# The rank features of a shared pass computed by quarters of its tokens, in the bank of the odd group's sums

## Chip, cores and metric

The kernel runs on one core of one Trainium2 chip. The metric is the device time of one execution in microseconds (us); lower is better.

## What is computed

The input is read as 2048 rows of 512. Each row is normalised, goes through an attention against a context, is added back and normalised again. A mixture of experts follows: each of the 2048 rows (tokens) goes to two of eight experts, and a shared expert sees all of them. Every expert, the shared one too, has a second, narrow branch of rank 32. For the shared one:

```python
sh = gelu(xt @ sw1 + sb1) @ sw2 + sb2      # 512 -> 2048 -> 512
sh = sh + gelu(xt @ swd) @ swu             # 512 -> 32 -> 512
out = out + 0.2 * sh
```

The change touches `gelu(xt @ swd)`, the rank features of the shared expert.

## The kernel before

**Staging.** Tokens are handled in 16 groups of 128. The first part of the kernel, up to about 640 us, runs attention and the shared expert together; the second part runs the eight experts. The shared expert works in 9 passes over tokens: pass 0 has group 0, passes 1 to 7 have groups 2p-1 and 2p (256 tokens), pass 8 has group 15. Between two passes lies a window of two groups' attention.

**Order.** Each of the five engines has its own program, and all walk the same list of units that `work_order()` writes out by hand. What an engine doesn't take part in it skips; what it does take part in it runs strictly in list order, waiting on semaphores. A pass p puts these units in the list, with pieces of attention between them: `rank` (the rank features), 16 times `up` (a block of 128 hidden features), and later `down` (hidden features times second weights). Just behind the second `up` the list has the last `values` unit of the odd group 2p+1 (L1776) and then its `ones` unit (L1785).

**Sums of the softmax.** For groups in `SUMMED` (2 and 4 to 15) VectorE adds up the exponentials in float32 (L1399, `late_stage`, 128x1024, in pairs of heads), and `ones` multiplies the total by a block of ones on TensorE. It waits for the last of those additions (`s_sum`). The result of an odd group goes to PSUM bank 3, that of an even group to bank 5. `den` reads it (L1411).

**A value in two parts.** Products run in bf16 with each float32 operand split into a high and a low part: three products for one. The rank weights are `wdh` and `wdl`. Before, each was stored three times side by side (96 columns, `WIDE`), so that one matmul gave three copies of the features on partitions 0 to 95 (L1822, 12 matmuls of 256 columns in a pass). ScalarE took the Gelu of all three copies at once (L1184), VectorE made the high part of all with one cast (L1487), and the low part of the middle copy with one subtraction (L1489). The tile `low` then holds high, low, high for `down` (L1849).

**The experts' way.** The rank features of the eight experts are already computed by quarters of the slots: 48 matmuls of 32 weight columns by 160 slots, each quarter on 32 partitions of its own (L1908), four Gelus (L1234), two casts and a subtraction (L1492, L1493, L1495).

**Banks.** `rank`, `up`, `down` and even `turn` units took PSUM banks 6 and 7 in turns (the function `shared_bank` waits for the reader of the unit that had the bank before). In the last `up` units of pass 7 and in pass 8 the ring is 6, 7, 0, 1. So before, the second `up` of a pass had the bank of `rank` and waited for its Gelu (`s_rgelu`).

Of the kernel before, what the change touches and what calls it, by code (L numbers as in the profile page):

```python
# [9 lines left out]
F32 = mybir.dt.float32  # L10
# [512 lines left out]
def build(nc, x, ctx_in, itok, gate_w, w1, b1, w2, b2, wd, wu, sw1, sb1, sw2, sb2, swd, swu, out):  # L523
    stack = ExitStack()
    with stack:
# [18 lines left out]
        wdf = sb("wdf", [P, KB, RANK], F32)  # L544
        wdh, wdl = sb("wdh", [P, KB, WIDE], BF16), sb("wdl", [P, KB, WIDE], BF16)
        wuf_turned, wus = sb("wuf_turned", [P, D], F32), sb("wus", [P, D], BF16)
# [6 lines left out]
        low = [sb(f"low{i}", [P, SLOTS], BF16) for i in range(2)]  # L553
        lowf = sb("lowf", [WIDE, SLOTS], F32)
        yout = [sb(f"yout{i}", [P, D], F32) for i in range(3)]
# [197 lines left out]


        shared_bank_of, shared_before, shared_unit, turn_bank, had, ring_turn = {}, {}, [], {}, {}, 0
        for unit in plan:
            if unit == ("place", 0):
                first_place = len(shared_unit)
            if (unit[0] in ("rank", "up") or (unit[0] == "down" and unit[3] == 0)
                    or (unit[0] == "turn" and unit[1] and unit[1] % 2 == 0)):  # L760
# [337 lines left out]
        def act_program(act):  # L1098
            act.wait_ge(s_pool, CONSTANTS)
            for unit in plan:  # L1100
# [76 lines left out]
                elif kind == "rank":  # L1177
# [5 lines left out]
                    w = P * len(groups_of(p))  # L1183
                    ac.activation(lowf[:, 0:w], bank(b)[0:WIDE, 0:w], ACT.Gelu).then_inc(s_rgelu, 1)  # L1184
                elif kind == "up":
# [112 lines left out]
        def dve_program(dve):  # L1298
# [9 lines left out]
            for unit in plan:  # L1308
# [148 lines left out]
                elif kind == "wd":  # L1457
                    e, n = unit[1], nth[unit]
                    dve.wait_ge(s_wd, 16 * n)
                    if e < E:  # L1460
                        dve.wait_ge(s_rank, PASSES + e)
                    copies = 3 if e == E else 1
                    for j in range(copies):
                        link(dv.tensor_copy(wdh[:, :, j * RANK:(j + 1) * RANK], wdf[:, :, :]))
                    dve.wait_ge(s_dve, chain)
                    for j in range(copies):
                        issued = dv.tensor_tensor(wdl[:, :, j * RANK:(j + 1) * RANK], wdf[:, :, :],
                                                  wdh[:, :, j * RANK:(j + 1) * RANK], ALU.subtract)
                        if j == copies - 1:
                            issued.then_inc(s_wdc, 1)  # L1470
                elif kind == "wu":
# [7 lines left out]
                elif kind in ("rank", "e_rank"):  # L1479
# [3 lines left out]
                    if m >= 2:  # L1483
                        dve.wait_ge(s_down, down_no(m - 2) if m - 2 < PASSES else e_down_no(m - 2 - PASSES, KB - 1))
                    if kind == "rank":
                        w = P * len(groups_of(m))
# [4 lines left out]
                    else:  # L1491
                        link(dv.tensor_copy(o[0:RANK, :], lowf[0:RANK, :]))  # L1492
                        link(dv.tensor_copy(o[2 * RANK:3 * RANK, :], lowf[0:RANK, :]))  # L1493
                        dve.wait_ge(s_dve, chain)
                        dv.tensor_tensor(o[RANK:2 * RANK, :], lowf[0:RANK, :], o[0:RANK, :], ALU.subtract).then_inc(s_low, 1)  # L1495
                elif kind == "up":
# [140 lines left out]
        def pe_program(pe):  # L1637
# [43 lines left out]
            for unit in plan:  # L1681
# [99 lines left out]
                elif kind == "ones":  # L1781
                    g = unit[1]
                    pe.wait_ge(s_sum, sum_no(g, QT - 1, 1))
                    for h in range(GH):
                        issued = mm(bank(3 if g % 2 else 5)[HD * h:HD * h + HD, :], ones_f[:, :], prob_sum[:, h * L:h * L + L],  # L1785
                                    start=True, stop=True)
# [25 lines left out]
                elif kind == "rank":  # L1812
# [3 lines left out]
                    pe.wait_ge(s_wdc, 1)  # L1816
                    b = shared_bank(unit)
                    n = 0
                    for weights, data in ((wdh, xth[p % 2]), (wdh, xtl[p % 2]), (wdl, xth[p % 2])):
# [64 lines left out]
                elif kind in ("e_rank", "e_up"):  # L1884
# [10 lines left out]
                    if kind == "e_rank":  # L1895
# [8 lines left out]
                        for weights, data in ((wdh, hi), (wdh, lo), (wdl, hi)):  # L1904
                            for kb in range(KB):
                                k += 1
                                for c in range(RANK_TILES):
                                    issued = mm(bank(b0)[c * RANK:(c + 1) * RANK, 0:RANK_COLS], weights[:, kb, 0:RANK],  # L1908
                                                data[:, kb, c * RANK_COLS:(c + 1) * RANK_COLS], start=k == 1, stop=k == 3 * KB)
# [107 lines left out]
```

## Time and profile before

| what | value |
| --- | --- |
| median of three runs | 1337.92 us (1335.53 to 1337.95) |
| the profiled execution | 1338.04 us |
| its span, first to last instruction | 1336.2 us |
| TensorE busy | 1293.7 us, 97% |
| VectorE busy | 841.5 us, 63% |
| ScalarE busy | 708.5 us, 53% |
| GpSimd busy | 253.1 us, 19% |
| mean granted TensorE clock | 0.987 of full speed |

The span is shorter than the execution by 1.8 us, which lie before the first and behind the last instruction. Busy shares are means over stages that have different limits, so what a change is worth is read from the stage in which it lies. In the rows below PE is TensorE, PEld its weight loads, DVE is VectorE, ACT ScalarE and POOL GpSimd. The ends of matmuls are modelled; the distance between starts is what counts for them.

### The profile page before, as it was taken

The numbers are of one execution on the slowest core, as the hardware profiler recorded it, in microseconds if no ns is written. First come the engines' busy times: TensorE is split into PE (matmuls) and PEld (weight loads), VectorE is DVE, ScalarE is ACT, GpSimd is POOL, SyncE is SP. The second block draws the span as 40 slices with busy tenths as digits, with TensorE's granted clock in tenths as the row PEclk, the third lists the DMA queues.
The fourth block names the chain that finished last, engine by engine and source line by source line (L and its number), as shares of the span: only waits on it lengthen the run. The fifth ranks groups of instructions, "written<-read, shape, count | busy, mean of one in ns | idle before, by whom it ended". The sixth has DMA issues, their size and how long they took to land.

```text
span 1336.2 us, 26800 instructions
## 1 busy us (share of the span) xinstructions
PE 1293.7 (97%) x10963; PEld 943.0 (71%) x11024; DVE 841.5 (63%) x1420; ACT 708.5 (53%) x1056; POOL 253.1 (19%) x219
## 2 busy tenths in 40 slices
PE   6788999999999999999999999999999999999997
PEld 2152736465554646384888889999999988888895
DVE  7777779797888887763742835638266383562730
ACT  5867676758676776662533524535244353442521
POOL 4740010000000051514200302203022030120112
PEclk7899999999999999999999999999999999999999
DMA  9614141423284332416736757677586775867313
GB/s 283 217 33 126 48 119 41 119 56 99 68 79 98 80 80 88 120 33 127 216 106 142 197 140 213 143 157 197 135 210 140 138 203 139 196 153 137 96 25 40
DMA packets 195627, 168.21 MB, mean 126 GB/s; under 512 B 117945, under 2 KB 138569, under 8 KB 195506
## 3 DMA queue, kind: packets, MB, share of 16 engines
q1 hardware_dynamic: 183218, 141.30, 40.7%
q0 software_dynamic: 12288, 25.21, 11.1%
q8 instruction: 87, 1.43, 0.5%
q14 instruction: 34, 0.28, 0.1%
HBM read 109.47 MB, written 34.15 MB: 107 GB/s over the span
## 4 chain that ended last, share of the span: by engine, by line
PE 88%; ACT 4%; issue 2%; DVE 2%; DMA 2%; SPq 1%; POOLq 0%; POOL 0%; another core or an unknown queue 0%; ACTq 0%; DVEq 0%
PE banks L1920 25%; PE banks L1950 24%; PE banks L1854 12%; PE banks L1836 10%; PE banks L1776 5%; PE banks L1756 4%; PE banks L1724 3%; ACT QS L1137 1%; DMA split_parts<-hidden 1%; PE banks L1810 1%; PE banks L1785 1%; ACT hf L1196 1%; ACT hidden L1150 1%; PE banks L1961 1%; PE banks L1822 1%
## 5 line engine op out<-in xcount | busy, mean ns | idle before, releaser
L1950 PE MATMUL banks<-hidden,w2h 128*128 128x0 bf16 x2048 | 306.1, 269 | 0.0
L1150 ACT ACTIVATE hidden<-banks,scales 128x512 f32<-128x512 f32 x256 | 170.4, 688 | 86.4 <-PE banks L1756 55.3
L1950 PEld LDWEIGHTS banks<-hidden,w2h 128*128 128x128 bf16 x2048 | 198.6, 98 | 20.5
L1378 DVE TENSOR_REDUCE rowmax<-banks 128x1 f32<-128x512 f32 x256 | 172.8, 686 | 33.0 <-PE banks L1724 31.6
L1950 PE MATMUL banks<-hidden,w2l 128*128 128x0 bf16 x1024 | 192.3, 269 | 0.0
L1529 DVE TENSOR_TENSOR w1l<-stage,w1h 128x2048 bf16<-128x2048 f32 x32 | 73.2, 2292 | 187.7 <-ACT w1h L1227 187.7
L1854 PE MATMUL banks<-w2h,hidden 128*128 128x512 bf16 x498 | 179.1, 379 | 0.8 <-issue 0.5
L1244 ACT ACTIVATE hf<-banks,b1cols 128x640 f32<-128x640 f32 x128 | 101.4, 793 | 122.4 <-PE banks L1920 108.8
L1255 ACT ACTIVATE yT<-banks 128x640 uint16<-128x640 uint16 x56 | 36.4, 702 | 215.2 <-PE banks L1950 215.2
L1920 PE MATMUL banks<-eth,w1h 128*128 128x0 bf16 x1024 | 133.0, 273 | 0.0
L1920 PE MATMUL banks<-etl,w1h 128*128 128x0 bf16 x1024 | 132.9, 273 | 0.0
L1920 PE MATMUL banks<-eth,w1l 128*128 128x0 bf16 x1024 | 132.9, 273 | 0.0
L1081 POOL DMA_INDIRECT xg<-normed_rows,slots x40 | 51.0, 1274 | 345.4 <-PE banks L1920 279.4
L1920 PEld LDWEIGHTS banks<-eth,w1l 128*128 128x128 bf16 x1024 | 100.1, 98 | 12.0
L1920 PEld LDWEIGHTS banks<-etl,w1h 128*128 128x128 bf16 x1024 | 100.1, 98 | 12.0
L1920 PEld LDWEIGHTS banks<-eth,w1h 128*128 128x128 bf16 x1024 | 99.4, 98 | 12.8
L1522 DVE TENSOR_TENSOR hidden<-hf,hidden 128x640 bf16<-128x640 f32 x128 | 105.7, 826 | 4.4
L1950 PEld LDWEIGHTS banks<-hidden,w2l 128*128 128x128 bf16 x1024 | 100.2, 98 | 10.3
L1196 ACT ACTIVATE hf<-banks,sb1cols 128x256 f32<-128x256 f32 (+1 forms) x144 | 64.6, 451 | 75.3 <-PE banks L1836 71.6
L1724 PE MATMUL banks<-KS,QS 96*128 96x512 bf16 x240 | 93.6, 393 | 9.0 <-DVE rowmax L1378 4.4
L1756 PE MATMUL banks<-QS,KS 128*128 128x512 bf16 x234 | 90.3, 388 | 9.5 <-ACT hidden L1150 6.3
L1093 POOL DMA_INDIRECT out_rows<-yout,slots x35 | 61.5, 1757 | 199.2 <-ACT yout L1269 132.9
(199 smaller groups left out, 1966.4 us busy)
## 6 DMA issues: line engine op xcount, KB each, us to landing
stage<-in_L_ffn_w SPq DMA_DIRECT2D x64, 1024.0 KB
split_parts<-hidden SPq DMA_DIRECT2D x16, 512.0 KB, 4.9
QS<-split_parts SPq DMA_DIRECT2D x48, 128.0 KB, 2.7
KS<-split_parts SPq DMA_DIRECT2D x48, 128.0 KB, 3.2
xin<-in_x SPq DMA_DIRECT2D x16, 256.0 KB, 3.8
cin<-in_ctx SPq DMA_DIRECT2D x16, 256.0 KB, 3.9
out_rows<-xin SPq DMA_DIRECT2D x16, 256.0 KB, 2.0
normed_rows<-x2r SPq DMA_DIRECT2D x16, 256.0 KB, 3.4
```

The source lines that it names most:

```text
L1150: ac.activation(prob[n % NPH], bank(score_bank[unit]), ACT.Exp, scale=scales[:, g // 2:g // 2 + 1]).then_inc(s_exp, 1)
L1196: ac.activation(h_out, bank(b)[:, 0:w], ACT.Gelu, bias=sb1cols[:, fb:fb + 1]).then_inc(s_gelu, 1)
L1244: ac.activation(by_choice(hf[n % 2][:, :]), PB[:, b0:b0 + 2, 0:CAP], ACT.Gelu, bias=b1cols[:, e * FB + fb:e * FB + fb + 1]).then_inc(s_gel ...
L1378: dv.reduce_max(rowmax[g % 2][:, i:i + 1], bank(score_bank[unit]), X_AXIS).then_inc(s_max, 1)
L1522: dv.tensor_tensor(hl[:, fb, :], hf[n % 2][:, :], hh[:, fb, :], ALU.subtract).then_inc(s_hl, 1)
L1529: dv.tensor_tensor(lo, stage[j % NST][:, :].rearrange("p (a w) -> p a w", w=512), hi, ALU.subtract).then_inc(s_wlo, 1)
L1724: mm(bank(score_bank[unit]), QS[s][0:96, h, t * P:t * P + P], KS[s][0:96, h, :], start=True, stop=True).then_inc(s_score, 1)
L1756: mm(bank(score_bank[unit]), KS[s][:, h, t * P:t * P + P], QS[s][:, h, :], start=True, stop=True).then_inc(s_st, 1)
L1836: issued = mm(bank(b)[:, 0:w], weights[:, kb, f0:f0 + P], data[:, kb, 0:w], start=n == 1, stop=n == 3 * KB)
L1854: issued = mm(bank(b_down), a[:, fb, cols], w[:, fb, :], start=False, stop=(fb, k) == (FB - 1, 2))
L1920: issued = mm(bank(b0 + j)[:, 0:CAP].shape_from_register(used_cols(e, j)), weights[:, kb, f0:f0 + P], of_choice(data[:, kb, :], j).shape_f ...
L1950: issued = mm(bank(b0 + j)[:, skips[j]:CAP].shape_from_register(used_cols(e, j)), w[:, fb, rows], of_choice(a[:, fb, :], j, skips[j]).shap ...
```

## The change

The rank features of a shared pass are computed as the experts' are. The weights are stored once (32 columns). The tokens of a pass are cut into four quarters of q (64, in passes 0 and 8 it is 32), and each of the 12 matmuls becomes four, one for each quarter, that write to partitions 0, 32, 64 and 96. ScalarE takes four Gelus, which put the quarters side by side on partitions 0 to 31. VectorE casts twice, since only one copy is left, and subtracts once. From pass 2 on `rank` leaves the ring of banks and takes bank 3; `ones` of an odd group now waits for its Gelu as well.

```diff
+        def rank_in_sums(p):
+            return p == PASSES - 1 or 2 * p + 1 in SUMMED
...
+            if unit[0] == "rank" and rank_in_sums(unit[1]):
+                shared_bank_of[unit] = 3
+            elif (unit[0] in ("rank", "up") or (unit[0] == "down" and unit[3] == 0)
...
-                    ac.activation(lowf[:, 0:w], bank(b)[0:WIDE, 0:w], ACT.Gelu).then_inc(s_rgelu, 1)
+                    q = w // RANK_TILES
+                    for c in range(RANK_TILES):
+                        issued = ac.activation(lowf[0:RANK, c * q:(c + 1) * q], bank(b)[c * RANK:(c + 1) * RANK, 0:q], ACT.Gelu)
+                    issued.then_inc(s_rgelu, 1)
...
-                    copies = 3 if e == E else 1
-                    for j in range(copies):
-                        link(dv.tensor_copy(wdh[:, :, j * RANK:(j + 1) * RANK], wdf[:, :, :]))
+                    link(dv.tensor_copy(wdh[:, :, :], wdf[:, :, :]))
...
-                        link(dv.tensor_copy(o[0:WIDE, 0:w], lowf[:, 0:w]))
-                        dve.wait_ge(s_dve, chain)
-                        dv.tensor_tensor(o[HD:2 * HD, 0:w], lowf[HD:2 * HD, 0:w], o[HD:2 * HD, 0:w],
-                                         ALU.subtract).then_inc(s_low, 1)
+                    link(dv.tensor_copy(o[0:RANK, 0:w], lowf[0:RANK, 0:w]))
+                    link(dv.tensor_copy(o[2 * RANK:3 * RANK, 0:w], lowf[0:RANK, 0:w]))
+                    dve.wait_ge(s_dve, chain)
+                    dv.tensor_tensor(o[RANK:2 * RANK, 0:w], lowf[0:RANK, 0:w], o[0:RANK, 0:w], ALU.subtract).then_inc(s_low, 1)
...
                     pe.wait_ge(s_sum, sum_no(g, QT - 1, 1))
+                    if g % 2:
+                        pe.wait_ge(s_rgelu, g // 2 + 1)
...
-                    b = shared_bank(unit)
+                    b = 3 if rank_in_sums(p) else shared_bank(unit)
+                    if p == PASSES - 1:
+                        pe.wait_ge(s_den, GROUPS)
...
-                            issued = mm(bank(b)[0:WIDE, 0:w], weights[:, kb, :], data[:, kb, 0:w], start=n == 1, stop=n == 3 * KB)
+                            for c in range(RANK_TILES):
+                                issued = mm(bank(b)[c * RANK:(c + 1) * RANK, 0:q], weights[:, kb, :],
+                                            data[:, kb, c * q:(c + 1) * q], start=n == 1, stop=n == 3 * KB)
```

The order of the engines changes at `rank` alone. On VectorE, at the rank unit of pass 3, the order before is (rowmax is the maximum over scores, late_stage the addition that `ones` waits for):

```order
L1378 TENSOR_REDUCE rowmax_72<-banks 128x1
L1487 CAST low<-lowf 96x256
L1489 TENSOR_TENSOR low<-lowf,low 32x256
L1378 TENSOR_REDUCE rowmax_72<-banks 128x1
L1399 TENSOR_TENSOR late_stage<-late_stage,hidden 128x1024
L1505 TENSOR_TENSOR hidden<-hf,hidden 128x256
```

And on VectorE at the same place with the change:

```order
L1387 TENSOR_REDUCE rowmax_72<-banks 128x1
L1489 CAST low<-lowf 32x256
L1490 CAST low<-lowf 32x256
L1492 TENSOR_TENSOR low<-lowf,low 32x256
L1387 TENSOR_REDUCE rowmax_72<-banks 128x1
L1408 TENSOR_TENSOR late_stage<-late_stage,hidden 128x1024
L1502 TENSOR_TENSOR hidden<-hf,hidden 128x256
```

One cast is added, ahead of the last addition; nothing changes places. On TensorE in the same pass, from the rank unit to the `ones` unit, with what each first instruction waits for, before:

```order
L1822 MATMUL banks<-xth_51,wdl 96x256 x4
L1724 MATMUL banks<-KS_62,QS_61 128x512 [waits s_exp]
L1836 MATMUL banks<-xth_51,w1h 128x256 [waits s_logit]
...
L1836 MATMUL banks<-xth_51,w1h 128x256 [waits s_rgelu]
...
L1776 MATMUL banks<-hidden,VT_70 32x512 [waits s_exp]
L1776 MATMUL banks<-hidden,VT_70 32x512 x3
L1785 MATMUL banks<-late_stage,ones_f 32x512 [waits s_sum]
```

And on TensorE with the change:

```order
L1825 MATMUL banks<-xth_51,wdl 32x64 x16
L1721 MATMUL banks<-KS_62,QS_61 128x512 [waits s_exp]
L1840 MATMUL banks<-xth_51,w1h 128x256 [waits s_y]
...
L1840 MATMUL banks<-xth_51,w1h 128x256 [waits s_logit]
...
L1773 MATMUL banks<-hidden,VT_70 32x512 [waits s_exp]
L1773 MATMUL banks<-hidden,VT_70 32x512 x3
L1784 MATMUL banks<-late_stage,ones_f 32x512 [waits s_rgelu,s_sum]
```

The wait for the rank features' Gelu moves from the second `up` to `ones`; the matmuls of the rank unit are four times as many and a quarter as wide.

## Rows read from the trace of the kernel before

**Rows 1.** The page: busy time of each engine.

```profile
PE 1293.7 (97%) x10963; PEld 943.0 (71%) x11024; DVE 841.5 (63%) x1420; ACT 708.5 (53%) x1056; POOL 253.1 (19%) x219
```

**Rows 2.** Busy time by stretch, window of pass 3; order PE, PEld, DVE, ACT, POOL.

```profile
281.00:353.00 72.00, 71.53 (x502) 40.24 (x506) 58.86 (x108) 50.43 (x88) 5.92 (x6) 1.00 0.33 82
```

**Rows 3.** Timeline, pass 3: start, us, engine, line; idle before it and releaser.

```profile
280.70 0.60 PE L1822 MATMUL banks<-xth,wdh 128*96 128x256 bf16 x4
...
282.01 0.38 PE L1724 MATMUL banks<-KS,QS 96*128 96x512 bf16 x1
...
282.68 0.38 ACT L1184 ACTIVATE lowf<-banks 96x256 f32<-96x256 f32 x1
282.69 0.69 DVE L1378 TENSOR_REDUCE rowmax<-banks 128x1 f32<-128x512 f32 x1
...
283.29 0.28 DVE L1487 CAST low<-lowf 96x256 bf16<-96x256 f32 x1
...
283.60 0.41 DVE L1489 TENSOR_TENSOR low<-lowf,low 32x256 bf16<-32x256 f32 x1
...
283.76 0.60 PE L1836 MATMUL banks<-xth,w1h 128*128 128x256 bf16 x4
...
284.77 1.23 DVE L1399 TENSOR_TENSOR late_stage<-late_stage,hidden 128x1024 f32<-128x1024 f32 x1
...
285.38 1.06 PE L1776 MATMUL banks<-hidden,VT 128*32 128x512 f32 x8
...
286.05 0.34 PEld L1785 LDWEIGHTS banks<-late_stage,ones_f 128*32 128x32 f32 x8 [0.52 <-DVE late_stage L1399]
...
286.26 1.04 PE L1785 MATMUL banks<-late_stage,ones_f 128*32 128x512 f32 x8
```

**Rows 4.** Groups by line and form on ScalarE: busy, mean ns | idle before.

```profile
L1184 ACT ACTIVATE lowf<-banks 96x256 f32<-96x256 f32 x7 | 2.7, 382 | 0.1
L1184 ACT ACTIVATE lowf<-banks 96x128 f32<-96x128 f32 x2 | 0.5, 265 | 2.7 <-PE banks L1822 2.7
```

**Rows 5.** Timeline, rank unit of expert 0 on three engines.

```profile
638.84 0.46 PE L1908 MATMUL banks<-eth,wdh 128*32 128x160 bf16 x16
...
639.78 1.08 PE L1920 MATMUL banks<-eth,w1h 128*128 128x0 bf16 x8
...
639.90 1.22 ACT L1234 ACTIVATE lowf<-banks 32x160 f32<-32x160 f32 x4 [0.36 <-PE banks L1908]
```

**Rows 6.** Timeline, pass 6, VectorE's cast, and values and ones on TensorE.

```profile
498.49 0.52 DVE L1487 CAST low<-lowf 96x256 bf16<-96x256 f32 x1
...
500.58 1.07 PE L1776 MATMUL banks<-hidden,VT 128*32 128x512 f32 x8
...
501.49 0.64 PE L1785 MATMUL banks<-late_stage,ones_f 128*32 128x512 f32 x4
```

**Rows 7.** Timeline, pass 7, the same place.

```profile
568.97 0.38 ACT L1184 ACTIVATE lowf<-banks 96x256 f32<-96x256 f32 x1
569.39 0.29 DVE L1487 CAST low<-lowf 96x256 bf16<-96x256 f32 x1 [0.86 <-ACT lowf L1184]
...
571.44 0.40 PEld L1785 LDWEIGHTS banks<-late_stage,ones_f 128*32 128x32 f32 x8 [0.46 <-DVE late_stage L1399]
...
571.71 1.04 PE L1785 MATMUL banks<-late_stage,ones_f 128*32 128x512 f32 x8
```

**Rows 8.** Timeline, pass 0 and what VectorE did for the rank weights.

```profile
43.80 1.66 DVE L1467 TENSOR_TENSOR wdl<-wdf,wdh 128x128 bf16<-128x128 f32 x3
...
74.45 1.15 DVE L1489 TENSOR_TENSOR low<-lowf,low 32x128 bf16<-32x128 f32 x1
...
76.38 0.39 PE L1724 MATMUL banks<-KS,QS 96*128 96x512 bf16 x1 [0.83 <-DVE rowmax L1378]
```

**Rows 9.** Timeline, pass 8, TensorE: four matmuls of 16 or 32 columns.

```profile
595.65 0.18 PE L1871 MATMUL banks<-b1rows,ones 128*128 128x16 bf16 x1 [0.41 <-DVE b1rows L1591]
...
595.77 0.38 PE L1836 MATMUL banks<-xth,w1h 128*128 128x128 bf16 x4
```

More of the change, by code:

```diff
@@ L544, in build @@
         wdf = sb("wdf", [P, KB, RANK], F32)
-        wdh, wdl = sb("wdh", [P, KB, WIDE], BF16), sb("wdl", [P, KB, WIDE], BF16)
+        wdh, wdl = sb("wdh", [P, KB, RANK], BF16), sb("wdl", [P, KB, RANK], BF16)
         wuf_turned, wus = sb("wuf_turned", [P, D], F32), sb("wus", [P, D], BF16)
@@ L553, in build @@
         low = [sb(f"low{i}", [P, SLOTS], BF16) for i in range(2)]
-        lowf = sb("lowf", [WIDE, SLOTS], F32)
+        lowf = sb("lowf", [RANK, SLOTS], F32)
         yout = [sb(f"yout{i}", [P, D], F32) for i in range(3)]
@@ L758, in build @@
                 first_place = len(shared_unit)
-            if (unit[0] in ("rank", "up") or (unit[0] == "down" and unit[3] == 0)
+            if unit[0] == "rank" and rank_in_sums(unit[1]):
+                shared_bank_of[unit] = 3
+            elif (unit[0] in ("rank", "up") or (unit[0] == "down" and unit[3] == 0)
                     or (unit[0] == "turn" and unit[1] and unit[1] % 2 == 0)):
@@ L1461, in dve_program @@
                         dve.wait_ge(s_rank, PASSES + e)
-                    copies = 3 if e == E else 1
-                    for j in range(copies):
-                        link(dv.tensor_copy(wdh[:, :, j * RANK:(j + 1) * RANK], wdf[:, :, :]))
+                    link(dv.tensor_copy(wdh[:, :, :], wdf[:, :, :]))
                     dve.wait_ge(s_dve, chain)
[L1466 to L1470, printed above, removed]
+                    dv.tensor_tensor(wdl[:, :, :], wdf[:, :, :], wdh[:, :, :], ALU.subtract).then_inc(s_wdc, 1)
                 elif kind == "wu":
@@ L1484, in dve_program @@
                         dve.wait_ge(s_down, down_no(m - 2) if m - 2 < PASSES else e_down_no(m - 2 - PASSES, KB - 1))
-                    if kind == "rank":
-                        w = P * len(groups_of(m))
-                        link(dv.tensor_copy(o[0:WIDE, 0:w], lowf[:, 0:w]))
-                        dve.wait_ge(s_dve, chain)
-                        dv.tensor_tensor(o[HD:2 * HD, 0:w], lowf[HD:2 * HD, 0:w], o[HD:2 * HD, 0:w],
-                                         ALU.subtract).then_inc(s_low, 1)
[L1491 to L1495, printed above, removed]
+                    w = P * len(groups_of(m)) if kind == "rank" else SLOTS
+                    link(dv.tensor_copy(o[0:RANK, 0:w], lowf[0:RANK, 0:w]))
+                    link(dv.tensor_copy(o[2 * RANK:3 * RANK, 0:w], lowf[0:RANK, 0:w]))
+                    dve.wait_ge(s_dve, chain)
+                    dv.tensor_tensor(o[RANK:2 * RANK, 0:w], lowf[0:RANK, 0:w], o[0:RANK, 0:w], ALU.subtract).then_inc(s_low, 1)
                 elif kind == "up":
@@ L1907, in pe_program @@
                                 for c in range(RANK_TILES):
-                                    issued = mm(bank(b0)[c * RANK:(c + 1) * RANK, 0:RANK_COLS], weights[:, kb, 0:RANK],
+                                    issued = mm(bank(b0)[c * RANK:(c + 1) * RANK, 0:RANK_COLS], weights[:, kb, :],
                                                 data[:, kb, c * RANK_COLS:(c + 1) * RANK_COLS], start=k == 1, stop=k == 3 * KB)
```

1 line of the change is left out of this document (added).

## The prediction, made before the changed kernel ran

> **What bounds the kernel now.** I read the page first: TensorE is busy 97% of the span, so a saving counts only if TensorE gets through its list sooner [rows 1]. Then the busy time by stretch. Between the rank units of pass 2 and pass 5 it repeats, and the window of pass 3 stands for it: of 72.0 us TensorE is busy 71.53, VectorE 58.86, ScalarE 50.43, at a granted clock of 1.00 [rows 2]. The reader is to see that nothing but TensorE is full over such a window. But a mean hides a short stretch in which another engine is full, so I went through the timeline of the stretch from the rank unit to `ones` [rows 3]. There VectorE has no gap: rowmax at 282.69, cast at 283.29, subtraction at 283.60, another rowmax, and the last addition from 284.77 to 286.00. The weight load of `ones` follows at 286.05, 0.05 us behind the addition and released by it, after the load side had stood idle for 0.52 us. Its matmul starts at 286.26, which is 0.88 us behind the start of `values` at 285.38.
>
> Was TensorE held up by that wait? In pass 6 the same distance, from 500.58 to 501.49, is 0.91 [rows 6], though nothing else is alike there, so about 0.88 is what the matmuls of `values` themselves take, and in pass 3 the wait is just covered. What is left as cover is the distance from the release to the matmul: 286.26 less 286.05 = 0.21 us. Passes 2 and 4 have the same rows, and pass 5 has 0.1 less. In pass 6 nothing is left, since 0.91 is already 0.03 more than what the matmuls need [rows 6]. In pass 7 it is 571.71 less 571.44 = 0.27 [rows 7]. So six times in the kernel TensorE meets an addition of VectorE with 0 to 0.27 us to spare, and the change puts its new work ahead of that addition.
>
> **TensorE's part of the change.** A rank unit of 256 tokens takes from 280.70 to the next matmul at 282.01, 1.31 us [rows 3]. With the change it has 48 matmuls of 64 columns. The nearest rows are the experts' 48 of 160 columns: all 48, from 638.84 to the next weights' matmul at 639.78, take 0.94 us, 20 ns each [rows 5]. If the columns alone counted, it would be 0.94 x 64/160 = 0.38. At the other end, full-width matmuls of only 16 or 32 columns start 30 ns apart (four from 595.65 to 595.77 [rows 9]), which would make 1.44. I take 0.85, nearest the experts' form, a little less for narrower data: a saving s of 0.45 us, bounds -0.13 to 0.93. The Trainium skill weighs against this step: "TensorEngine Tiling (Array Packing)", section Instruction Overhead, gives each matmul about 60 cycles whatever its width and advises not to take the tiling factor from a dimension that is already small. By that, and at 2.4 GHz, 48 would take an estimated 1.2 us and save 0.1. The experts' rows, 20 ns for each of 48, don't show such a floor where four quarters overlap; those of 30 ns apart do.
>
> **ScalarE's part.** One Gelu of 96x256 takes 0.382, of 96x128 0.265 [rows 4]: 0.91 ns a column, so 64 columns take 0.207. The experts' four of 160 columns take 1.22 together, 0.305 each, where the same slope gives 0.294 for one; the gap is some 0.015 [rows 5]. Four of 64 make 4 x 0.207 + 3 x 0.015 = 0.87, which is 0.49 more than the 0.38 of now. Bounds: 0.75 if narrow ones overlap, 1.22 if they cost as the experts' do.
>
> **VectorE's part.** The added cast costs the distance from cast to subtraction, 283.60 less 283.29 = 0.31 [rows 3]; it has the same 256 columns. The first cast must also wait for the later Gelu. In pass 3 the Gelus run from 282.68 to 283.55 and the cast follows 0.04 later, as in pass 7 (568.97 + 0.38 to 569.39 [rows 7]): 283.59 for 283.29, 0.30 late. Together the addition ends 0.61 late, at 286.61, and the matmul of `ones` can start some 0.06 later, 286.67. Before it was 286.26: **0.41 us lost**. TensorE arrives s earlier than before, but it must stand and wait there, since its list is in order; the whole saving goes into that wait. Nothing refunds the loss, because TensorE is full over the rest of the window. Late next are `den`, the third `up` and all behind them, by the same amount. VectorE's scores and subtractions of hidden features have their own slack there.
>
> The passes one by one. Passes 2 to 5 are alike: 4 x 0.41 = 1.64. In pass 6 the cast took 0.52, not 0.28, so up to 0.24 of the lateness falls into what held that cast; with 0.01 of cover, 0.61 - 0.24 - 0.01 = 0.36 [rows 6]. In pass 7 the cast waited for the Gelu already (idle 0.86), so all 0.49 counts: 0.49 + 0.31 - 0.27 = 0.53 [rows 7]. Sum 2.53.
>
> **Pass 1** has no `ones` and keeps the ring, so its second `up` still waits for the Gelu. In pass 3, and just so in pass 1, that `up` starts at 283.76, 0.70 behind the Gelu's end at 283.06 [rows 3]; with the Gelus 0.49 longer and 0.06 from release to matmul, it can come no more than 0.15 sooner, whatever s is. Gain 0.15. **Pass 8**, with 32 columns, takes 0.1 more or less than now on TensorE, but TensorE stands 0.41 us for VectorE's routing a little later [rows 9], which hides it: 0. If that cover were gone it would be 0.1. **Pass 0** is the least sure. Its Gelus end some 0.5 later, a cast of 0.25 is added, and TensorE already waits 0.83 for VectorE just behind [rows 8]; that would lose 0.55. Against it, the three subtractions of the weights at 43.80 (1.66 us) become one. If the work behind them, and with it GpSimd's splitting of weights, is done some 1.1 us earlier, the subtraction at 74.45, which took 1.15 where the one of twice the columns takes 0.41 [rows 3], runs free, and pass 0 gains 0.3. I take a gain of 0.1. The bank leaves no new wait: bank 3 was last read for the rows that ScalarE copied before the exponentials, and `ones` waits for the Gelus at 283.55, long before the addition.
>
> **Sum**, against the profiled execution of 1338.04 (span 1336.2 and 1.8 around it, 0.1 above the median): 2.53 - 0.15 - 0.1 = 2.3, so **1340.3 us**. A measurement of this kernel tells about 0.2% (2.7 us) from no change, and this lies just inside.
>
> **Rivals.**
> 1. *The saving is kept.* If the addition of VectorE doesn't hold `ones`, each pass from 1 to 7 is worth s: 7 x 0.45 = 3.2, so 1334.9, and 1331.5 with the upper bound of s. It needs the addition to end at least 0.25 us earlier than now rather than 0.6 later; the point from which it decides is a lateness below the cover of 0.21. For it speaks only that VectorE has 13 us to spare in a window [rows 2]; against it, that these are elsewhere.
> 2. *The delay is absorbed.* Something later in each window that doesn't move with TensorE (a transfer, ScalarE's exponentials) has it waiting anyway, and takes in the 0.4 us. Then the time stays at 1338 to 1339. Against it speaks the 71.53 of 72.0 us.
> 3. *More is lost.* If a Gelu of 64 columns on 32 partitions costs what one of 160 does (1.22 for four), the lateness grows by 0.35 in each of six passes, 2.1 us; 1342.4. If narrow matmuls start 30 ns apart [rows 9], 48 take 1.44 us: some 0.8 more than now in passes 0 and 8 (12 matmuls of half the columns, 1.31/2), of which pass 8 hides 0.41, and 0.13 in pass 1 in place of its gain; with 0.8 + 0.4 + 0.3 on top, 1341.8. This is the floor's way, and a third of this rival's chance is its. The page quoted above is what speaks for it most.
>
> **How the numbers follow.** The forecast's mechanism has 0.52, with a range of its own of 1339.0 to 1341.7 (the lateness 0.15 less or more in six passes, pass 0 from 0.3 gained to 0.55 lost); rival 1 has 0.10, rival 2 0.18, rival 3 0.20. Over 0.2% slower is above 1340.6: nearly half of the first (0.24) and almost all of rival 3 (0.19), 0.43. Faster is rival 1, 0.10. The rest, 0.47, is no change that can be told. The range takes the first and second and most of the third: 1336.6 to 1342.9.
>
> **What would show it.** Right: in passes 2 to 7 the load side idles for about 1.4 us ahead of `ones` (0.52 + 0.41 + s), released by the addition, and the matmul of `ones` starts some 1.7 us behind that of `values` instead of 0.88 (0.88 + 0.41 + s); the window from rank to rank grows by 0.4 from 71.7 us; the four Gelus take 0.87 together; the two casts start 0.31 apart. Wrong: a distance of 0.88 there, with shorter windows (rival 1), or longer distances with windows of 71.7 us (rival 2). The start-up could mislead me, where the clock is not yet at its upper level and small shifts may move it.

## The result, and the profile after

The changed kernel took 1341.69 us (median of 10; 1338.98 to 1347.43), the kernel before 1336.41 (median of 10 on the same chip; 1334.45 to 1338.09). The ratio is 1.0046, 95% interval 1.003 to 1.0062: slower by more than the 0.2% that can be told. The profiled execution took 1341.79 us, its span is 1340.0.

The page, busy time of each engine. TensorE works 4.4 us less than in [rows 1] and the kernel is slower all the same, so the loss is waiting:

```profile
PE 1289.3 (96%) x11287; PEld 936.0 (70%) x11348; DVE 843.0 (63%) x1425; ACT 710.8 (53%) x1083; POOL 252.3 (19%) x219
```

Busy time of the window of pass 3, from its rank unit to the next (PE, PEld, DVE, ACT, POOL). TensorE is busy 70.68 of 72.06 us, where [rows 2] have 71.53 of 72.0:

```profile
281.43:353.49 72.06, 70.68 (x536) 38.95 (x540) 58.85 (x108) 50.48 (x91) 5.92 (x6) 1.00 0.34 81
```

The timeline of pass 3, which answers to [rows 3]:

```profile
281.12 0.38 PE L1721 MATMUL banks<-KS,QS 96*128 96x512 bf16 x1
...
281.43 0.30 PE L1825 MATMUL banks<-xth,wdh 128*32 128x64 bf16 x16
...
281.56 0.29 PE L1825 MATMUL banks<-xtl,wdh 128*32 128x64 bf16 x16
...
281.92 0.39 PE L1721 MATMUL banks<-KS,QS 96*128 96x512 bf16 x1
...
283.32 0.90 ACT L1192 ACTIVATE lowf<-banks 32x64 f32<-32x64 f32 x4
...
284.25 0.28 DVE L1489 CAST low<-lowf 32x256 bf16<-32x256 f32 x1 [0.23 <-ACT lowf L1192]
...
284.56 0.28 DVE L1490 CAST low<-lowf 32x256 bf16<-32x256 f32 x1
...
284.88 0.41 DVE L1492 TENSOR_TENSOR low<-lowf,low 32x256 bf16<-32x256 f32 x1
...
285.33 0.69 DVE L1387 TENSOR_REDUCE rowmax<-banks 128x1 f32<-128x512 f32 x1
...
285.93 1.22 DVE L1408 TENSOR_TENSOR late_stage<-late_stage,hidden 128x1024 f32<-128x1024 f32 x1
...
286.07 0.10 PEld L1721 LDWEIGHTS banks<-KS,QS 96*128 96x128 bf16 x1 [1.20 <-DVE rowmax L1387]
286.08 0.39 PE L1721 MATMUL banks<-KS,QS 96*128 96x512 bf16 x1 [0.92 <-DVE rowmax L1387]
...
286.40 1.07 PE L1773 MATMUL banks<-hidden,VT 128*32 128x512 f32 x8
...
287.20 0.21 PEld L1784 LDWEIGHTS banks<-late_stage,ones_f 128*32 128x32 f32 x8 [0.65 <-DVE late_stage L1408]
...
287.28 1.04 PE L1784 MATMUL banks<-late_stage,ones_f 128*32 128x512 f32 x8
```

Three things are to be seen. **The saving is larger than forecast.** From the start of the rank unit to the next matmul it is 281.92 - 281.43 = 0.49 us, for 1.31 before: 0.82 saved, where 0.45 was taken. Sixteen of the narrow matmuls take 0.13 us from the first start to the seventeenth, 8 ns each in the mean. Ahead of the unit 0.09 is given back: it starts 0.31 behind the score, not 0.22. **TensorE doesn't keep it.** It waits 0.92 us, one unit earlier than the prediction had it: not at `ones`, but at a score (L1721) that stands ahead of `values`. The score needs the bank that a rowmax of VectorE reads, and that rowmax (285.33 to 286.02) comes straight behind the two casts and the subtraction. In the timeline of the kernel before the same two instructions stand like this, with no wait:

```profile
284.05 0.69 DVE L1378 TENSOR_REDUCE rowmax<-banks 128x1 f32<-128x512 f32 x1
...
285.07 0.38 PE L1724 MATMUL banks<-KS,QS 96*128 96x512 bf16 x1
```

With the change `ones` follows `values` by 0.88 us, as before. **The windows are longer all the same.**

The starts of the rank units give all the windows (us):

| from rank unit to rank unit | before | changed |
| --- | --- | --- |
| start to 1 | 137.30 | 137.34 |
| 1 to 2 | 71.70 | 72.05 |
| 2 to 3 | 71.70 | 72.04 |
| 3 to 4 | 71.70 | 72.06 |
| 4 to 5 | 71.72 | 72.08 |
| 5 to 6 | 71.77 | 72.13 |
| 6 to 7 | 70.88 | 71.16 |
| 7 to 8 | 25.63 | 26.09 |
| 8 to the first `down` of pass 7 | 14.83 | 15.87 |
| from there to the end of the span | 729.0 | 729.2 |

The windows of passes 1 to 7 grow by 0.35, 0.34, 0.36, 0.36, 0.36, 0.28 and 0.46, together 2.5 us. The end of pass 8 loses 1.0, the rest 0.2: with the 2.5 that is the 3.8 by which the two spans differ. The medians differ by 5.3.

### The profile page after: what moved, and what is told of

Read it like the earlier page. It is cut to its first block, busy times and chain, and to the rows that moved or that the text cites. A ratio compares the mean times of both kernels' runs of the same rounds, so it can differ in the third digit from the quotient of the medians.

```text
span 1340.0 us, 27486 instructions
## 1 busy us (share of the span) xinstructions
PE 1289.3 (96%) x11287; PEld 936.0 (70%) x11348; DVE 843.0 (63%) x1425; ACT 710.8 (53%) x1083; POOL 252.3 (19%) x219
## 4 chain that ended last, share of the span: by engine, by line
PE 86%; ACT 5%; issue 3%; DVE 3%; DMA 1%; SPq 1%; another core or an unknown queue 0%; POOLq 0%; POOL 0%; ACTq 0%; DVEq 0%
PE banks L1924 25%; PE banks L1954 24%; PE banks L1858 12%; PE banks L1840 8%; PE banks L1773 5%; PE banks L1753 4%; PE banks L1721 3%; ACT QS L1143 1%; DVE rowmax L1387 1%; ACT hf L1205 1%; PE banks L1784 1%; ACT hidden L1156 1%; PE banks L1809 1%; PE banks L1965 1%; ACT L1192 1%
## 5 line engine op out<-in xcount | busy, mean ns | idle before, releaser
L1721 PE MATMUL banks<-KS,QS 96*128 96x512 bf16 x240 | 94.0, 394 | 14.0 <-DVE rowmax L1387 10.4
```

The lines of the kernel that those rows point to most:

```text
L1721: mm(bank(score_bank[unit]), QS[s][0:96, h, t * P:t * P + P], KS[s][0:96, h, :], start=True, stop=True).then_inc(s_score, 1)
```

## The experiments

Two theories for the windows: **VectorE is late** (the Gelus end later, and one more cast stands ahead of the rowmax), or **the bank or the number of instructions** (bank 3, the shifted ring, 48 matmuls for 12). The first four kernels ran on one chip, where the kernel before took 1333.66 us (median of 35).

**One more cast, alone.** In the kernel before, the cast is cut in two by partitions:

```diff
-  link(dv.tensor_copy(o[0:WIDE, 0:w], lowf[:, 0:w]))
+  link(dv.tensor_copy(o[0:2 * HD, 0:w], lowf[0:2 * HD, 0:w]))
+  link(dv.tensor_copy(o[2 * HD:WIDE, 0:w], lowf[2 * HD:WIDE, 0:w]))
```

> The kernel before, with its one cast of the rank features cut into two of the same width (partitions 0 to 63, then 64 to 95). If VectorE's lateness is what costs time: the chain up to the last addition ends 0.31 us later, some 0.17 to 0.2 of it is covered, so each of the windows of 71.7 us grows by 0.1 to 0.15, and pass 0 by up to 0.25: 0.8 to 1.2 us in all, 1337.4. If it is not VectorE but the matmuls, the bank or the ring of banks that costs time: no change, windows of 71.7.

1336.25 us, ratio 1.0014 (1.0004 to 1.0025). Its windows from pass 1 on are 71.68, 71.80, 71.81, 71.82, 71.96, 71.14 and 25.58: 0.1 more in passes 2 to 4, 0.2 in 5, 0.26 in 6 and nothing in 1 and 7. Its timeline in pass 3 has the wait at the score, at its very threshold (0.16 us of idle loads):

```profile
283.18 0.28 DVE L1487 CAST low<-lowf 64x256 bf16<-64x256 f32 x1
...
283.49 0.28 DVE L1488 CAST low<-lowf 32x256 bf16<-32x256 f32 x1
...
284.25 0.69 DVE L1378 TENSOR_REDUCE rowmax<-banks 128x1 f32<-128x512 f32 x1
...
285.00 0.10 PEld L1725 LDWEIGHTS banks<-KS,QS 96*128 96x128 bf16 x1 [0.16 <-DVE rowmax L1378]
```

One cast's 0.31 costs about 0.1, because the rest was cover. So the cast is a part of the loss and not all of it. The windows add up to 0.7 us, and the medians are 2.6 apart: most of that difference lies outside the windows and isn't explained. The profile's start-up is longer too (the rank unit of pass 1 starts at 137.11, for 135.08 and 135.35 in the next two kernels), but that is one profile of each.

**Four Gelus, alone.** In the kernel before, each Gelu takes a quarter of the columns of all 96 partitions:

```diff
-  ac.activation(lowf[:, 0:w], bank(b)[0:WIDE, 0:w], ACT.Gelu).then_inc(s_rgelu, 1)
+  q = w // RANK_TILES
+  for c in range(RANK_TILES):
+      issued = ac.activation(lowf[:, c * q:(c + 1) * q], bank(b)[0:WIDE, c * q:(c + 1) * q], ACT.Gelu)
+  issued.then_inc(s_rgelu, 1)
```

> The kernel before, with its one Gelu of the rank features cut into four of a quarter of the columns, 96 partitions each. VectorE's lateness: the Gelus end 0.5 us later, the cast behind them 0.30 later, the windows grow by 0.1 to 0.15 as with two casts (0.3 in pass 7), 0.8 to 1.3 us in all, 1337.4. The other theories: no change.

1334.13 us, ratio 1.0002 (0.9993 to 1.001), windows of 71.68 to 71.71 in passes 1 to 4. That doesn't clear the Gelus, since this kernel didn't make the cast behind them late: it starts 2.58 us behind the rank unit's start, for 2.59 before. Its timeline:

```profile
280.43 0.56 ACT L1186 ACTIVATE lowf<-banks 96x64 f32<-96x64 f32 x4
...
281.04 0.28 DVE L1490 CAST low<-lowf 96x256 bf16<-96x256 f32 x1
```

Here the four take 0.56 us together, and those of the changed kernel 0.90. One Gelu takes the same in both, 0.21 to 0.23 us. What differs is the distance from one start to the next: 0.10 to 0.12 here, where they overlap, and 0.225 in the changed kernel, where each waits for the end of the one before. The two kernels differ in the number of partitions, in where the Gelus read and in where they write, and no run tells these apart. The experiment missed what it was made for, so the Gelus' share was never tested by itself.

**The bank, alone.** The kernel before, with the rank units of passes 2 to 8 in bank 3, and so the ring of the changed kernel:

```diff
+            if unit[0] == "rank" and rank_in_sums(unit[1]):
+                shared_bank_of[unit] = 3
...
+                    if g % 2:
+                        pe.wait_ge(s_rgelu, g // 2 + 1)
...
-                    b = shared_bank(unit)
+                    b = 3 if rank_in_sums(p) else shared_bank(unit)
+                    if p == PASSES - 1:
+                        pe.wait_ge(s_den, GROUPS)
```

> The kernel before, with the rank features of passes 2 to 8 in bank 3 and its waits, nothing by quarters. VectorE's lateness: windows of 71.7 us, no change there. The ring of banks: with one unit less in it, the first down unit of pass 7 gets the bank of up unit 14 of pass 8 rather than of up unit 12, and waits for its Gelu; up to 1 us more from the rank unit of pass 8 (14.8 us now) to that down unit, 1336.5 to 1337.5 in all.

1334.09 us, ratio 1.0001 (0.9993 to 1.001), windows of 71.68 to 71.71 in passes 1 to 4. The bank alone costs nothing on this chip. Up to 1 us more was expected in the stretch from the rank unit of pass 8 to the first `down` of pass 7; it took 12.43 us, for 12.28 and 12.29 in the two kernels above.

**All but the bank.** The changed kernel with every rank unit in the ring (the wait of pass 8's unit for `s_den`, which bank 3 needs, goes with it):

```diff
         def rank_in_sums(p):
-            return p == PASSES - 1 or 2 * p + 1 in SUMMED
+            return False
```

> The changed kernel with its rank units in the ring of banks as before; all else by quarters. VectorE's lateness: windows of 72.0 us as in the changed kernel, so 2.5 us more than before from there, and the stretch from the rank unit of pass 8 to the first down unit back at 14.8 us: 1339 to 1340, about 1 to 2 below the changed kernel. If bank 3 and its waits were what costs in each window: windows of 71.7 or less, and 1336 or less.

1336.84 us, ratio 1.0029 (1.0018 to 1.004), and its windows in passes 1 to 4 are 72.05 to 72.07, those of the changed kernel to 0.01. Its timeline on TensorE in pass 3:

```profile
284.04 0.61 PE L1838 MATMUL banks<-xth,w1h 128*128 128x256 bf16 x4 [0.43 <-ACT lowf L1192]
...
285.84 0.39 PE L1721 MATMUL banks<-KS,QS 96*128 96x512 bf16 x1 [0.32 <-DVE rowmax L1387]
```

In the ring TensorE waits first for the Gelus and then for the rowmax, out of it only for the rowmax, and the window comes out alike: the last wait of the stretch sets it. The windows' loss is not the bank's.

The next four ran on another chip, where the kernel before took 1336.35 us (median of 23). The first is the changed kernel itself, for comparison.

> The changed kernel once more, to stand beside the three below on one chip. Windows of 72.05 us, 0.2 to 0.4% over the kernel before. The windows explain 2.5 us of it; if the ratio is again nearer 0.5%, something outside the windows costs the rest in most executions.

1346.29 us (six executions, 1341.36 to 1347.23), ratio 1.0063 (1.0046 to 1.0079). The profiled one took 1341.60 and has windows of 72.06 to 72.15 in passes 1 to 5.

**The second cast out of the way.** In the changed kernel it moves behind the subtraction of hidden features of `up` 12 (of `up` 15 in pass 8), since `down` needs it only then:

```diff
-                    link(dv.tensor_copy(o[2 * RANK:3 * RANK, 0:w], lowf[0:RANK, 0:w]))
...
+                    if fb == (12 if p < PASSES - 1 else FB - 1):
+                        lw = P * len(groups_of(p))
+                        dve.wait_ge(s_dve, chain)
+                        dv.tensor_copy(low[p % 2][2 * RANK:3 * RANK, 0:lw], lowf[0:RANK, 0:lw]).then_inc(s_low, 1)
```

> The changed kernel, with the second cast of a shared pass (the third copy) moved on VectorE to behind up unit 12 of the pass (15 in pass 8). VectorE's lateness: the chain up to the last addition is 0.31 us shorter, so its lateness falls from 0.61 to about 0.3, and the windows from 72.05 to between 71.7 and 71.8; 1.7 to 2.5 us less than the changed kernel. Were the four Gelus alone to blame: 72.05 as it is.

1340.41 us, ratio 1.0024 (1.0016 to 1.0033). The windows of passes 1 to 4 are 71.72 to 71.75: the whole 0.31 of a cast comes back, since behind a wait without cover each 0.1 us of VectorE is 0.1 of the window. TensorE's wait at the score falls by as much, from 0.92 to 0.61 us:

```profile
285.03 0.28 DVE L1489 CAST low<-lowf 32x256 bf16<-32x256 f32 x1 [0.23 <-ACT lowf L1192]
...
286.54 0.39 PE L1730 MATMUL banks<-KS,QS 96*128 96x512 bf16 x1 [0.61 <-DVE rowmax L1387]
```

The windows are within 0.05 us of those before but for pass 7 (0.15 more), 0.3 us in all, and the kernel is still 4.1 us slower in the medians. So nearly all of what is left of the loss lies outside the windows.

**All three out of the way.** In the changed kernel both casts and the subtraction move to the same place:

```diff
-                elif kind in ("rank", "e_rank"):
-                    m = unit[1] if kind == "rank" else PASSES + unit[1]
+                elif kind == "rank":
+                    continue
+                elif kind == "e_rank":
+                    m = PASSES + unit[1]
...
+                    if fb == (12 if p < PASSES - 1 else FB - 1):
+                        o, lw = low[p % 2], P * len(groups_of(p))
+                        dve.wait_ge(s_rgelu, p + 1)
+                        if p >= 2:
+                            dve.wait_ge(s_down, down_no(p - 2))
+                        link(dv.tensor_copy(o[0:RANK, 0:lw], lowf[0:RANK, 0:lw]))
+                        link(dv.tensor_copy(o[2 * RANK:3 * RANK, 0:lw], lowf[0:RANK, 0:lw]))
+                        dve.wait_ge(s_dve, chain)
+                        dv.tensor_tensor(o[RANK:2 * RANK, 0:lw], lowf[0:RANK, 0:lw], o[0:RANK, 0:lw], ALU.subtract).then_inc(s_low, 1)
```

> The changed kernel, with both casts and the subtraction of a shared pass moved on VectorE to behind up unit 12 (15 in pass 8). If VectorE's work ahead of the last addition is all that eats the saving of the matmuls (1.53 us from score to score around the rank unit before, 0.80 after), it comes out now: windows of 71.0 us (71.70 less 0.73), 5 us less than before in seven of them, 0.3 to 0.4% faster than before. If TensorE is held there by something else as well (the Gelus, the start of the next up unit), windows of 71.3 to 71.7 and no more than 0.2% faster. Pass 1 keeps its wait for the Gelus and stays at 71.6.

1331.76 us, ratio 0.9958 (0.9943 to 0.9973): faster than both kernels. Passes 2 to 5 have windows of 70.95 to 71.04, so 0.7 us below the kernel before and 1.1 below the changed one. Its timeline in pass 3 has no wait at the score, nor at `ones`, which starts 4.75 us behind the rank unit for 5.56 before and 5.85 with the change:

```profile
276.82 0.30 PE L1836 MATMUL banks<-xth,wdh 128*32 128x64 bf16 x16
...
278.71 0.90 ACT L1192 ACTIVATE lowf<-banks 32x64 f32<-32x64 f32 x4
278.72 1.28 DVE L1387 TENSOR_REDUCE rowmax<-banks 128x1 f32<-128x512 f32 x2
...
279.92 1.22 DVE L1408 TENSOR_TENSOR late_stage<-late_stage,hidden 128x1024 f32<-128x1024 f32 x1
...
280.38 0.38 PE L1732 MATMUL banks<-KS,QS 96*128 96x512 bf16 x1
...
281.57 1.04 PE L1795 MATMUL banks<-late_stage,ones_f 128*32 128x512 f32 x8
```

Here the saving reaches the windows and the time: 0.82 less the 0.09 ahead of the rank unit is 0.73, and the windows give 0.73 to 0.75. Pass 1, whose second `up` has the bank of the rank unit, has 71.55 and gains just the 0.15 that the prediction allowed a pass in the ring. Passes 1 to 7 gain 4.8 us together, and the medians are 4.6 apart.

**The same move in the kernel before.** Is it the move that gains, or the change together with it? One cast and the subtraction move, at the kernel before:

```diff
+                        link(dv.tensor_copy(o[0:WIDE, 0:lw], lowf[:, 0:lw]))
+                        dve.wait_ge(s_dve, chain)
+                        dv.tensor_tensor(o[HD:2 * HD, 0:lw], lowf[HD:2 * HD, 0:lw], o[HD:2 * HD, 0:lw],
+                                         ALU.subtract).then_inc(s_low, 1)
```

> The kernel before, with its cast and subtraction of a shared pass moved in the same way. VectorE's chain was just covered there, so its shortening gives TensorE nothing: windows of 71.70 us and no change within 0.1%. If they shrink, VectorE held TensorE before already, and the gain of the late work in the changed kernel is not that of its shorter matmuls.

1335.34 us, ratio 0.999 (0.998 to 1.0), windows of 71.69 to 71.72 in passes 1 to 4. Without the change TensorE was just not waiting for VectorE, so VectorE's earliness is worth nothing. Only both together gain more than can be mistaken.

### The rest of the loss

The windows explain 2.5 us, and the medians are 4.9 to 9.9 apart in the three groups of runs that have the changed kernel. The end of pass 8 was the next place to look. Three kernels ran on a third chip (before: 1335.68, median of 19): the changed kernel with only pass 8's rank unit back in the ring, again without that wait for `s_den`,

```diff
         def rank_in_sums(p):
-            return p == PASSES - 1 or 2 * p + 1 in SUMMED
+            return p < PASSES - 1 and 2 * p + 1 in SUMMED
```

> The changed kernel with one thing put back: the rank unit of pass 8 takes its bank from the ring, as before, so down of pass 7 gets the bank it had before the change. Passes 2 to 7 keep bank 3. Known so far: the windows explain 2.5 us of the loss, the stretch from the rank unit of pass 8 to the first down of pass 7 took 15.9 us with the change and 12.2 where the rank units stay in the ring, and the changed kernel has executions near 1341 and near 1347. Theory: the rest of the loss is the end of pass 8, where the rank unit left the ring. Then this comes out near the quarters in the ring on the same chip (e10), 1.002 to 1.004 of the kernel before, with that stretch at 12 to 13 us and no execution 5 us above the others. Rival 1, the bank of passes 2 to 7 or the number of instructions: it stays at 1.0045 to 1.006 with some executions 5 us higher. Rival 2, the stretch differs from chip to chip, not from kernel to kernel: then e10 and this have the longer stretch both.

then the kernel with all of them in the ring, and the changed one.

> The kernel of e4 once more (the changed kernel with every rank unit in the ring), now on the chip of e9 and e11. If the ring is what keeps the end of pass 8 short, 12.2 us from the rank unit of pass 8 to the first down of pass 7 and 1.002 to 1.004 of the kernel before. If the stretch belongs to the chip, 15 us or more and a ratio like that of e11.

> The changed kernel itself, on the chip of e9 and e10. If the ring is the cause of the rest: 1.0045 to 1.0065 of the kernel before, some executions near 1346, and 15 us or more at the end of pass 8, while e9 and e10 lie 0.2% below it. If it is the chip: the same ratio as e10.

| kernel | us | ratio | rank unit of pass 8 to first `down` |
| --- | --- | --- | --- |
| last one in the ring | 1341.82 | 1.0044 (1.003 to 1.0059) | 15.12 |
| all in the ring | 1339.06 | 1.0026 (1.0013 to 1.0039) | 13.91 |
| changed | 1340.56 | 1.0047 (1.0028 to 1.0066) | 15.71 |

Neither stands as it was put, the theory that pass 8's unit out of the ring is the cause, nor its rival that the stretch belongs to the chip alone. Putting the last unit back gained nothing, and the stretch of the kernel with all in the ring is longer than on the first chip (13.91 for 12.19). But putting it back is no return to the old banks. With six units out of the ring the rank unit of pass 8 gets the bank of `up` 14 of pass 7 and waits for its Gelu, and the second `up` behind it gets the rank unit's own:

```profile
595.81 0.28 PE L1823 MATMUL banks<-xth,wdh 128*32 128x32 bf16 x16 [0.90 <-ACT hf L1205]
...
597.66 0.40 PE L1838 MATMUL banks<-xth,w1h 128*128 128x128 bf16 x4 [0.55 <-ACT lowf L1192]
```

So this kernel pays 1.0 us that the table doesn't show, in the window ahead of the rank unit of pass 8 (27.07 us, for 26.09 and 26.10 in the two others), and it was no clean test of that unit.

Two things lie in the stretch. The first is a piece in which TensorE waits for nothing that the profile shows, put down to "issue", in the last `up` units of pass 8 (the short piece, below). Every profiled execution on the chip of the result and on those of the second and third group has it, whatever the kernel, and none of the four of the first group does. On TensorE, all in the ring:

```profile
606.24 0.28 PE L1838 MATMUL banks<-xth,w1h 128*128 128x128 bf16 x2 [0.16 <-issue]
...
606.94 0.38 PE L1838 MATMUL banks<-xtl,w1h 128*128 128x128 bf16 x4 [0.42 <-issue]
...
607.69 0.33 PE L1838 MATMUL banks<-xth,w1l 128*128 128x128 bf16 x3 [0.32 <-issue]
...
608.21 0.38 PE L1851 MATMUL banks<-wus,low 128*128 128x512 bf16 x1 [0.19 <-issue]
```

The second is the bank of the first `down` of pass 7. With all in the ring it is the bank of `up` 12 of pass 8. In the changed kernel it is that of `up` 14, and with only the last unit put back it is still that of `up` 14, which is a second reason why putting it back undid nothing. The changed kernel on the same chip:

```profile
606.31 0.38 PE L1840 MATMUL banks<-xtl,w1h 128*128 128x128 bf16 x4 [0.39 <-issue]
...
607.04 0.33 PE L1840 MATMUL banks<-xth,w1l 128*128 128x128 bf16 x3 [0.29 <-issue]
...
609.40 0.38 PE L1853 MATMUL banks<-wus,low 128*128 128x512 bf16 x1 [2.03 <-ACT hf L1205]
```

`down` there waits 2.03 us for a Gelu of hidden features, and 0.19 with all in the ring. The short piece lengthens this wait as well, since it holds ScalarE too:

```profile
608.52 0.88 ACT L1205 ACTIVATE hf<-banks,sb1cols 128x128 f32<-128x128 f32 x3 [1.80 <-PE banks L1840]
```

The last three Gelus of pass 8 come in one run, 1.15 us behind the end of the last `up` matmul; in the five profiles without the piece the last one starts 0.04 behind it. Where the short piece is missing, `down` hardly waits: the kernel with the bank alone takes 12.43 us for the stretch, on the first chip. So the shifted ring costs up to 1.8 us where the short piece stands ahead of it, and 0.2 at most elsewhere. That rests on one profile of each, and the intervals of 1.0026 and 1.0047 overlap.

**What stays open.** The 24 timed executions of the changed kernel in the three groups fall into two kinds: 14 from 1338.7 to 1343.0, 10 from 1344.9 to 1347.4. All three that were profiled are of the lower kind. The bank isn't needed for such a gap: of the 12 executions with all in the ring on the first chip, two took 1341.4 at a mean granted clock of 0.991, the others 1335.1 to 1339.5. With the second cast late none of 12 took more than 1342.4. One more execution of the changed kernel was profiled, on a chip that no other experiment had:

> One more execution of the changed kernel, for its trace. Of 24 executions so far 9 took 1344.9 to 1347.4 us, the others 1338.7 to 1343.0, and only the lower kind has been profiled. If this one is of the upper kind, the theory is a granted clock of half speed over some 10 us more in a stretch that TensorE bounds, likeliest right behind the idle piece at the end of pass 8 (608 to 612 us), where the kernel with the second cast late had 0.50; the windows of the passes stay at 72.05. Rival: longer windows at full clock. If it is of the lower kind, it shows windows of 72.05 again and nothing more.

(It is ten, not nine, of the upper kind.) This took 1336.12 us, and one execution of the kernel before beside it 1334.33. It is of neither kind: its windows in passes 1 to 5 are 72.06 to 72.14 again, the end of pass 8 is 12.33, with no short piece. Nine of the ten upper ones have a mean granted clock of 0.990 to 0.992. Most of the lower ones have 0.994 to 0.996, though some have 0.991 or 0.992 too. One profile shows what such a clock can do at the costly place: that of the kernel with the second cast late, in the stretch behind the short piece (the column behind TensorE's busy time is its granted clock):

```profile
608.00:610.00 2.00, 0.49 (x3) 0.91 0.01 1
610.00:612.00 2.00, 1.63 (x4) 0.50 0.02 0
612.00:614.00 2.00, 2.00 (x8) 0.74 0.75 11
```

TensorE had idled before it (busy 0.49 of 2.00 us), its clock is granted at 1.2 GHz, the lower of its two levels, for some 3 us, and the first `down` matmuls start 0.43 us apart instead of 0.21. From the first `down` to the experts' rank unit this execution takes 32.9 us for 31.6. Whether the upper kind is a longer piece of this, nothing here shows. So of the 5.3 us between the medians the windows' 2.5 are explained, the end of pass 8 has about 1, and how the rest is shared between the upper kind and the scatter of the start-up is not settled. The cause is shown for the windows and not for the whole time.

## Why the prediction was right, and where not

- **What bounds the kernel**: right. TensorE sets the windows, and what made it late was VectorE without a gap in one short stretch, where the means show 13 us to spare.
- **TensorE's saving, 0.45 us taken**: too small; 0.82, inside the bounds of -0.13 to 0.93. The unit takes 0.49 us to the next matmul, for 0.85 taken and 0.38 "if the columns alone counted". Its matmuls start in sets: the four quarters 3 to 4 ns apart, and most sets 29 ns behind the one before. With the 32 columns of pass 8 most are 25 ns apart, with the experts' 160 columns 70. The Trainium skill gives each matmul about 60 cycles ("TensorEngine Tiling (Array Packing)", Instruction Overhead), at 2.4 GHz an estimated 25 ns. The trace agrees for a set of four (25 ns with 32 columns, where half of the 29 of 64 columns would be 15), and not for 48 matmuls one behind another, as the prediction reckoned it (1.2 us). The rows of 30 ns at full width were no neighbour either, since nothing overlaps there. As the prediction said, the size of the saving made no difference to the windows: they grew by the delay of VectorE's chain, and the saving went into the wait.
- **ScalarE's four Gelus, 0.87**: 0.90 measured. In pass 3 the first starts 1.89 us behind the rank unit's start (1.98 before), the cast 2.82 behind it (2.59 before), with 0.23 of idle time for the Gelus.
- **VectorE's second cast, 0.31**: 0.31 measured, both as a distance and as what its removal gives back.
- **Where the wait stands, at `ones`, released by the addition**: wrong in passes 2 to 6. This is the step that failed: the path was right in its engine and wrong in its instruction. The prediction followed VectorE's last addition to `ones` and passed over the rowmax ahead of it, for whose bank the score ahead of `values` waits. That rowmax moved from 3.35 to 3.90 us behind the rank unit's start. The score of before started at 285.07, 0.33 behind the rowmax's end (284.05 + 0.69), and starts 0.06 behind it now, so its cover was 0.27: 0.55 - 0.27 = 0.28, and with the 0.09 ahead of the rank unit about the 0.35 that the windows show. The signature given (1.7 us from `values` to `ones`) didn't come: it is still 0.88. The idle time of the load side, 1.4 forecast, came in two pieces, 1.20 and 0.65. In pass 7 the wait does stand at `ones` (1.11 us, released by the addition).
- **Passes 2 to 5, 0.41 each**: 0.34 to 0.36. **Pass 6, 0.36**: 0.28. **Pass 7, 0.53**: 0.46. Together 2.53 forecast, 2.16 measured.
- **Pass 1, a gain of 0.15**: wrong, a loss of 0.35. It has no `ones`, but it has the score: since its rank unit is still in the ring, TensorE waits there 0.43 us for the Gelus and then 0.32 for the rowmax. The timeline of the changed kernel in pass 1:

```profile
140.18 0.61 PE L1840 MATMUL banks<-xth,w1h 128*128 128x256 bf16 x4 [0.43 <-ACT lowf L1192]
...
141.98 0.39 PE L1721 MATMUL banks<-KS,QS 96*128 96x512 bf16 x1 [0.32 <-DVE rowmax L1387]
```

  This error and those of the other passes cancel: 2.38 forecast for passes 1 to 7, 2.51 measured.
- **Pass 0, a gain of 0.1**: nothing to be told. Start to the rank unit of pass 1 took 137.30 before and 137.34 after; over all profiles, of all kernels, it lies between 134.3 and 138.8.
- **Pass 8, nothing**: about right for the unit itself (0.46 us to the next matmul, for 0.67; the wait for VectorE's routing behind it grew from 0.41 to 0.51), but the sentence "the bank leaves no new wait" looked at bank 3 alone. It missed that a unit taken out of the ring shifts the bank of every unit behind it, and that the first `down` got a bank read 1 to 2 us later. That costs about 1 us in the profiled pair, together with the short piece.
- **The time**: 1340.3 forecast for 1341.69, inside both ranges but above the nearer sum, and of the three outcomes it was slower (0.43) and not the likelier "no change" (0.47). Against the profiled execution of before the forecast was 2.3 us up, and the profiled one of after is 3.75 up; of the 1.4 between, the end of pass 8 is 1.0. That the number came within 1.4 us is luck in part: the forecast was counted from 1338.04, which is 1.6 above the median of the ten executions before, and between the medians the loss is 5.3 us, more than twice the 2.3. The sum for the windows was right for a reason that was partly wrong, too, since the first wait stands elsewhere and pass 1's error filled up what the others lacked. Rival 1 is out as the change stood, though it is what the kernel with the late casts does, windows 0.75 shorter. Rival 2 is out by windows that grew 0.35, rival 3 by four Gelus of 0.90 together and by a rank unit of 0.49, though its times of 1341.8 and 1342.4 lie as near to the measured one as the forecast does: the time alone wouldn't have told them apart.

## What to carry to other kernels

When work is added to an engine that has no gap in a stretch, list every instruction behind it that another engine waits for, with its cover in the trace, and not only the last one: here the first wait stood one unit earlier, and it was in all the passes. A saving on the bounding engine ahead of such a wait is worth nothing until the waited-for engine is relieved too: the change alone lost 0.5 to 0.6%, the move alone gained at most 0.2%, and both together gained 0.4%. And taking a unit out of a rotation of buffers shifts all the units behind it, so write out who had whose buffer, before and after.

## What the runs showed of the hardware

- Matmuls of 32 weight columns in four quarters of 32 partitions overlap: the four of a set start 3 to 4 ns apart. The next set mostly starts 25 ns later with 32 data columns (pass 8), 29 ns later with 64 (pass 3) and 70 ns later with 160 (the experts). All 48 of 64 columns start within 0.36 us.
- Four Gelus of 64 columns, each from 32 partitions of its own to partitions 0 to 31, start 0.225 us apart and take 0.90 us together. Four that read and write the same 96 partitions start 0.10 to 0.12 apart and take 0.56. One takes 0.21 to 0.23 in both; which of the differences keeps the first four from overlapping is not shown.
- In the last `up` units of pass 8, TensorE stood idle for 0.2 to 1.0 us at a time without a wait that the profile shows, in every profile of the result and on two chips of the experiments, and in none on two other chips. The changed kernel is among both. ScalarE's last Gelus came up to 1.2 us late in the same stretch. The traces don't show what the engines were short of.
